# Layer 1 of a graph network: the edge product is added to keys and values in SBUF for every second block

## The reference

```python
q = (x @ Wq.T + bq).reshape(n, HEADS, OUT_CH)      # k and v alike
e = (edge_attr @ We.T).reshape(-1, HEADS, OUT_CH)  # 50000 x 64 times 64 x 256
k_e = k[src] + e
v_e = v[src] + e
alpha = jnp.einsum('ehc,ehc->eh', q[dst], k_e) / jnp.sqrt(jnp.float32(OUT_CH))
m = jax.ops.segment_max(alpha, dst, num_segments=n)
p = jnp.exp(alpha - m[dst])
s = jax.ops.segment_sum(p, dst, num_segments=n)
w = p / (s[dst] + 1e-16)
out = jax.ops.segment_sum(v_e * w[:, :, None], dst, num_segments=n)
out = out.reshape(n, HC) + (x @ Wskip.T + bskip)
```

## Time and profile before

| | |
|---|---|
| median of 3 runs | 3405.53 us |
| the profiled execution | 3400.86 us, span 3399.1 us |
| layer 1's edge loop, first and last sum (L1343) | 913.3 to 1868.2 us |
| instructions of PE, DVE, POOL in the span | 13058, 5727, 1759 |
| busy share of the span, PE, DVE, ACT, POOL | 75%, 68%, 49%, 46% |

### The profile page before, as it was taken

The page is one execution under the profiler, slowest core; times in us unless marked ns, Lnnn a source line. Parts: engine busy times, 40 slices in busy tenths (PEclk is TensorE's granted clock), DMA queues, the critical chain, the costliest instruction groups (busy, mean ns, idle before and its releaser), DMA issues. The chain is left out here.

```text
span 3399.1 us, 57507 instructions
## 1 busy us (share of the span) xinstructions
PE 2549.1 (75%) x13058; PEld 1931.2 (57%) x13059; DVE 2318.5 (68%) x5727; ACT 1682.1 (49%) x4017; POOL 1550.8 (46%) x1759
## 2 busy tenths in 40 slices
PE   2999998428899999999997348888781368888770
PEld 1888887313566666666665246666661256666660
DVE  4777777465577877777775637767678546666677
ACT  1656555201454554545553246666661256666651
POOL 1323332100444545544541067777760077777740
PEclk9999999769899999999998667878786767877885
DMA  2100000121565555555562145555541155555521
GB/s 72 17 9 8 10 8 8 42 58 61 168 162 155 154 154 153 161 147 158 156 161 54 31 140 138 138 137 138 138 111 31 51 157 144 141 140 144 139 76 38
DMA packets 186285, 348.91 MB, mean 103 GB/s; under 512 B 74085, under 2 KB 116478, under 8 KB 185951
## 3 DMA queue, kind: packets, MB, share of 16 engines
q0 software_dynamic: 83520, 249.39, 29.1%
q1 hardware_dynamic: 102685, 98.62, 10.2%
HBM read 325.45 MB, written 22.44 MB: 102 GB/s over the span
## 5 line engine op out<-in xcount | busy, mean ns | idle before, releaser
L1620 POOL DMA_INDIRECT t_rows<-table_h,t_istage x896 | 853.3, 952 | 266.0 <-issue 251.0
L1206 POOL DMA_INDIRECT b_rows<-table_kv,b_istage x448 | 480.2, 1072 | 391.1 <-PE b_pso L1343 268.2
L1707 PE MATMUL t_pso<-t_rows,t_hot 125*125 125x272 f32 (+1 forms) x1792 | 594.7, 487 | 71.6 <-DVE t_rows L1746 36.8
L1707 PEld LDWEIGHTS t_pso<-t_rows,t_hot 125*125 125x125 f32 x1792 | 399.8, 235 | 168.9 <-issue 73.0
L1268 ACT COPY b_asked<-b_psq 125x512 f32<-125x512 f32 x224 | 131.1, 585 | 471.1 <-PE b_psq L1307 471.1
L1746 DVE TENSOR_TENSOR t_rows<-t_rows,t_psm 125x1056 f32<-125x1056 f32 x224 | 276.6, 1235 | 32.9 <-issue 32.8
L1693 PE MATMUL t_pss<-node_scores,t_hot_t 125*125 x1792 | 271.5, 282 | 33.3 <-ACT t_hot_t L1651 30.9
L1693 PEld LDWEIGHTS t_pss<-node_scores,t_hot_t 125*125 125x125 f32 x1792 | 265.6, 228 | 48.5 <-issue 43.6
L1658 ACT ACTIVATE t_hot<-con_iota,g_dstl 125x125 f32<-125x125 f32 x896 | 280.3, 384 | 0.0
L1756 DVE TENSOR_TENSOR acc<-acc,t_pso 125x272 f32 (+1 forms) x448 | 192.3, 429 | 121.2 <-DVE acc L1756 70.6
L1307 PE MATMUL b_psq<-queries,b_hot_t 125*125 x896 | 235.1, 385 | 45.3 <-issue 26.7
(11 more groups left out here) (392 smaller groups left out, 5190.6 us busy)
## 6 DMA issues: line engine op xcount, KB each, us to landing
t_places<-targets SPq DMA_DIRECT2D x56, 488.3 KB
t_rows<-table_h,t_istage POOLq DMA_INDIRECT x896, 3.7
b_attr<-in_attr_t SPq DMA_DIRECT2D x224, 62.5 KB
b_places<-targets SPq DMA_DIRECT2D x28, 488.3 KB
b_rows<-table_kv,b_istage POOLq DMA_INDIRECT x448, 5.5
table_h<-d_stage SPq DMA_DIRECT2D x50, 132.8 KB
t_flag<-flags SPq DMA_DIRECT2D x56, 62.5 KB
table_kv<-d_moved SPq DMA_DIRECT2D x25, 128.9 KB
```

The costliest lines, as they stand in the source:

```text
L1206: pool.indirect_dma_start(out=rows[:, h, s, :], out_offset=None, in_=table, in_offset=bass.IndirectOffsetOnAxis(ap=istage[:, h, s:s + 1], ...
L1620: pool.indirect_dma_start(out=rows[:, r, s, :], out_offset=None, in_=table, in_offset=bass.IndirectOffsetOnAxis(ap=istage[:, r, s:s + 1], ...
L1707: mm = pe.matmul(ps_o[b % 2][0:P, at:at + mw], hot[:, r, b * G + u, :], rows[0:P, r, b * G + u, 0:mw], start=u % PAIR == 0, stop=u % PAIR ...
```

## The change

In the blocks 1 and 3 of every chunk (`IN_ROWS`), the four identity matmuls are left out, and TensorE's `keys` no longer waits for the gathers: `ps_k` holds the edge product alone. VectorE's `offer` waits for the gathers instead, adds `ps_k` onto the gathered keys in `rows`, and then multiplies those with `asked`, in place, so that both inputs and the output are in SBUF; `judge` reads `asked`. The addition onto the values moves to GpSimd (`value`): one addition of key columns onto value columns in `rows`, behind the gathers of a block 0 (for block 1) and of a block 2 (for block 3). `message` of these blocks waits for it. The blocks 0 and 2 are as before.

```diff
+    IN_ROWS = (1, 3)
...
+        def in_rows_through(c, b):
+            return c * len(IN_ROWS) + sum(k <= b for k in IN_ROWS)
...
+                def value(c, h, b):
+                    pool_wait(pool, used, c * B + b + 1)
+                    mine = rows[0:P, h, b * G:(b + 1) * G]
+                    v = mine[:, :, D:].rearrange("p u (h c) -> p u h c", h=H)[:, :, :, 0:C]
+                    pool.tensor_tensor(v, v, mine[:, :, 0:D].rearrange("p u (h c) -> p u h c", h=H), ALU.add).then_inc(valued, 1)
...
                             pool.indirect_dma_start(...).then_inc(gathered[h * B + b], 16)
+                        behind_it = block_at(c, h, b + 1 - B)
+                        if behind_it and behind_it[2] in IN_ROWS:
+                            value(*behind_it)
...
                 def ask(c, h, b, v):
-                        act.wait_ge(used, n - 1)
+                        act.wait_ge(scored if b % 2 in IN_ROWS else used, n - 1)
...
                 def keys(c, h, b):
+                    apart = b in IN_ROWS
                     pe.wait_ge(attrset[b], c * 16 * GP + 16 * GP)
-                    pe.wait_ge(gathered[h * B + b], (c - h) * 8 * G + 16 * G)
+                    if not apart:
+                        pe.wait_ge(gathered[h * B + b], (c - h) * 8 * G + 16 * G)
...
-                            pe.matmul(to(v * PAIR + w), attr[half, b, w * P:(w + 1) * P], we[half], start=True, stop=False)
-                        for v in range(GP):
+                            mm = pe.matmul(to(v * PAIR + w), attr[half, b, w * P:(w + 1) * P], we[half], start=True, stop=apart)
+                        for v in range(0 if apart else GP):
...
                 def offer(c, h, b):
-                    dve.wait_ge(copied, (n + 1) * GP)
...
+                    if b in IN_ROWS:
+                        dve.wait_ge(gathered[h * B + b], (c - h) * 8 * G + 16 * G)
+                        keys = mine[:, :, 0:D]
+                        dve.tensor_tensor(keys, keys, k.rearrange("p (u d) -> p u d", u=G), ALU.add).then_inc(used, 1)
+                        dve.wait_ge(copied, (n + 1) * GP)
+                        dve.wait_ge(used, n + 1)
+                        dve.tensor_tensor(asked[:, b % 2], keys, asked[:, b % 2], ALU.mult).then_inc(multiplied, 1)
+                        return
+                    dve.wait_ge(copied, (n + 1) * GP)
...
                 def judge(c, h, b):
-                    products = rows[0:P, h, b * G:(b + 1) * G, 0:D].rearrange("p u (h c) -> p u h c", h=H)
+                    products = asked[:, b % 2] if b in IN_ROWS else rows[0:P, h, b * G:(b + 1) * G, 0:D]
+                    products = products.rearrange("p u (h c) -> p u h c", h=H)
...
                 def message(c, h, b):
-                    dve.wait_ge(used, n + 1)
+                    if b in IN_ROWS:
+                        dve.wait_ge(valued, in_rows_through(c, b))
+                    else:
+                        dve.wait_ge(used, n + 1)
```

More of the change, by code:

```diff
@@ L1153, in blend_phase @@
         distant, mset, summed, added, dv, rescaled = (sem(n) for n in ("distant", "mset", "summed", "added", "dve", "rescaled"))
+        valued = sem("valued")
         gathered = [sem(f"gathered{k}") for k in range(2 * B)]
@@ L1207, in body @@
                                                     in_offset=bass.IndirectOffsetOnAxis(ap=istage[:, h, s:s + 1], axis=0)).then_inc(gathered[h * B + b], 16)
+                        behind_it = block_at(c, h, b + 1 - B)
+                        if behind_it and behind_it[2] in IN_ROWS:
+                            value(*behind_it)
                 stage(0, 0)
                 halves(pool, body)
+                for b in range(1, B):
+                    if b in IN_ROWS:
+                        value(CHUNKS - 1, 1, b)
             @block.sync
```

## The result

The changed kernel takes 3503.3 us (median of 4 runs, 3498.8 to 3510.5) against 3405.1 (3399.1 to 3406.4): ratio 1.029, 95% interval 1.0275 to 1.0312. It is slower. Forecast were +73 us, measured +98.

What follows compares the result with a forecast made beforehand. The prediction took a ring of waits in layer 1's edge loop, not TensorE, as the bound. Terms: 0 identity products + 13 addition + 65 clock - 5 run-up = 73 us, giving 3479 us; range for 8 in 10: 3400 to 3520.

Steps and rivals of the forecast that it cites:

- the ring: Layer 1's edge loop: waits from queries through slot 3's and slot 0's sums, gathers and keys back to queries, 34.6 us a chunk.
- 119 us: TensorE's identity products over 56 blocks of layer 1's loop; taken as 0 won, 119 if the ring did not hold.
- The run-up: Six blocks before the first sum, three of them changed, with no ring: up to 3 x 2.1 us won, 5 taken.
- The clock: Layer 1's loop: TensorE, idle more often, gets a lower clock; 65 us lost, bounds 0 and 108.
- one visit a chunk: A stretch of TensorE at clock 0.50 behind the chunk's boundary pause, costing 2.4 us, between 1.4 and 4.0.
- 12 to 13 us: Sign: the step from slot 3's sum to slot 0's sum after the change, 9.94 us in the ring before.
- 0.80 to 0.92: Sign: the granted clock of layer 1's loop after the change, in the windows view; 0.99 before.
- fall as in layer 2: Rival: the clock falls as in layer 2's loop, or two visits a chunk, with longer scan wait; 3540 us, chance 0.13.
- clock holds: Rival: TensorE's clock in layer 1's loop does not fall, leaving 13 - 5; 3414 us, chance 0.20.
- TensorE is the bound: Rival: at slot 3's sum and slot 2's keys half the identity saving, 60 us, passes; 3346 us, chance 0.12.
- GpSimd's addition: Slot 3: 2.0 us long behind `message`, holding the port and moving the scan L1468 by 0.5 us a chunk, 13 us.
- what the prediction had named as its error: Sign of being wrong: the addition holds up `message` and not the scan, 2 us in the ring each time.

Runs made afterwards that it cites:

- e8: The changed kernel with GpSimd's addition for block 3 three blocks later in its program, off slot 3's `message`, nothing left out; ratio 1.017.
- e5: The changed kernel with GpSimd's addition cut to one element and TensorE given 8 dummy matmuls in place of the identity matmuls in blocks 1 and 3; ratio 1.005.
- e1: The changed kernel with GpSimd's addition cut to a single element; on another chip, ratio 1.024.
- e9: The change in blocks 0 and 2 instead of 1 and 3, GpSimd's additions one block later, the second only after VectorE's scans; ratio 0.999.
- e4: The changed kernel with each of GpSimd's additions one block later; on another chip, ratio 1.028.
- e2: The changed kernel with dummy matmuls, as many as the removed identity products, overwritten at once by the edge products; on another chip, ratio 1.030.
- e3: The kernel before, identity products kept, plus an unused GpSimd addition of the same size at the changed kernel's places; on another chip, ratio 1.018.
- c_after: The changed kernel unaltered, run again as reference on the chips of the later runs; ratio 1.032.
- e6: The same change made in blocks 0 and 2 instead of 1 and 3; ratio 1.010.
- e10: e9 with 8 dummy matmuls ahead of the edge products of blocks 0 and 2, where the identity matmuls stood; ratio 0.998.
- e7: The kernel before with 20 small VectorE memsets after the blend's last sum, putting later loops at the changed kernel's program places; ratio 1.005.

## Why the prediction was right, and where it was not

**No link of the ring holds an identity product: right.** TensorE's missing work made step 1 shorter (7.9 to 6.2 us) and step 2 longer by the same: the two together 16.3 before, 16.4 in e8. The keys of slot 2 wait for the gathers with 2.1 us idle, as forecast. Nothing of 119 us was won. The run-up, from the edge phase's first instruction to the first sum, won 5.6 us (59.4, not 65.0), forecast 5.

**The clock: right in kind and about in size.** Forecast were 65 us. With the port free, it is 1025.7 us from the first sum to the last with TensorE's work missing (e8) and 953.8 with it (e5): 72. e5 lacks the addition as well, but e1, which lacks it too, has a chunk of 37.6 us to e8's 37.4, so that is not what differs. The forecast priced one visit a chunk at 2.4 us in the step to slot 0's sum, "12 to 13 us"; e8 shows it there, 12.3 against 9.7. In the changed kernel itself that step is only 10.8, because of the next point. The loop's clock, 0.89, lies in the 0.80 to 0.92 named (the busy share that I had reasoned from is no safe guide to it, as e9 shows); it did not fall as in layer 2, and the rivals "clock holds" and "TensorE is the bound" fall.

**GpSimd's addition: right in length, wrong in what it holds up.** I took 2.0 us; it takes 2.28. The Trainium skill's figure (GPSIMD Engine Reference, "Elementwise — side-by-side cycle accounting"), halved, had given 2.25, and the trace agrees. The step that failed is the order: I let the addition start 0.30 us behind the last gather, when `message` would hold the port, and then delay the scan L1468 by 0.5 us (by the forecast's own rows it would have been 0.3). The 0.30 us lie between two gathers; there is none between a gather and an addition (gather to 1355.91, addition from 1355.92). `message` had no more than 0.28 us of a start by its record, and lost. The 0.30 us would not have saved it: with them it would have been 0.55 us ahead, and in e4 messages that were 0.47 to 0.62 us ahead were held up too. What was wrong is that so small a start keeps the port for VectorE. That is what the prediction had named as its error: `message` held up by 2.1 us, in the ring each time. The Trainium skill (SBUF — State Buffer, "Who interferes with whom") lets the first to issue keep the pair; that GpSimd's addition can hold up VectorE is shown, who issued first the records don't tell.

**The sum: the two costs are not added.** Port alone (e2, e3) makes a chunk of 38 us, clock alone (e8) 37.4, both 38.3 or 38.4. The wait for `message` is itself an idle time of TensorE and brings the half clock with it; and, as I read the steps, half clock that passes while TensorE waits costs nothing more. So the port adds 20 us to e8's 1086.4 (27 by c_after's 1113.8) and not 2.1 x 26 = 55; the forecast's 13 was too small by 7 to 14. That it was so near is luck: it priced a delay of the scan, which did not come to pass, and the one that did, 2.1 us of `message`, was mostly covered by half clock that was there anyway.

**What no step had: 16 us in layer 2,** from the place of a loop in VectorE's program. 13 + 65 - 5 = 73 became, in the profile, 84 in the edge phase (20 + 72 - 6 = 86 by the experiments), 16 in layer 2 and 4 elsewhere. The misses all point one way: 7 us of the addition, 7 of the clock, 16 and 4 outside the loop.

## What to carry to other kernels

An engine that is busy 94% of the time need not be on the path, and the work taken from it may be what keeps its clock up: look for where it would stand idle and what starts right behind. Before putting an elementwise operation on GpSimd, list VectorE's operations with two inputs in SBUF around its place and put it beside those that read PSUM. When phases that the change doesn't touch grow, look at the loop branches before looking for a mechanism.

## What the runs showed of the hardware

- GpSimd's addition (fp32, 125 x 1024, two inputs in SBUF; 2.17 us when free) delays VectorE's operations with two SBUF inputs from 1.25 to 3.5 us, and a tensor_scalar of 0.16 to 2.4, but not those with one input in PSUM (1.20 and 1.21 beside it in e9).
- Who waits, by the records of the changed kernel, e4, e6 and e8: where VectorE's operation starts 0.16 to 0.62 us ahead of the addition, VectorE waits (3.5 to 3.9 us, ending 1.1 us after the addition; 62 times); where it starts 0.69 us or more ahead, it keeps its 1.25 us and the addition takes 2.3 to 2.6 (61 times). The exceptions stand at the loop's end: three times an operation only 0.04 us ahead kept its time, and once in e6 one 1.7 us ahead did not. Why the border lies there is open.
- VectorE's loop branch costs 0.2 us or, by place alone, mostly 6 to 7.5 us (3.0 to 8.3). Layer 2's loop, 303 instructions, was quick where it began at instruction 1548 to 1565 of its program (before, e3, e8, e6, e9, e10) and slow at 1568 (changed, e1, e2, e4, e5, e7); layer 3's, 292 long, quick at 2602 and slow at 2618 (e8) and beyond. Layer 3's phase hardly grew all the same (599 to 601 us in each), except on the chip of e1 to e4 (742 us in e3, 754 to 759 in the others): what has the time there stays open. The Trainium skill (Runtime: NRT & Kernel Launch, "Instruction fetch mechanics") says that a taken branch to a target outside the two blocks held must fetch it again. A loop somewhat longer than one block would then fit in two or need three, by its place. That 3 instructions decide, 1565 or 1568, agrees with such a border; where the blocks begin, and the fetch itself, are in no record. What makes the loop L932 turn in 1.61, 1.63, 1.73 or 1.85 us stays open.
